# Quantised row tiles of a feed-forward network: transposed by DMA instead of by TensorE and ScalarE, with filler matmuls where TensorE waits

## The reference

```python
x = x + tanh(g_xattn) * xattn(layernorm(x), ctx)          # x is (2, 2048, 512), ctx is (2, 77, 512)
x = x + tanh(g_ffn) * ffn(layernorm(x))

def ffn(x, clip_x, clip_down, w_gate, w_up, w_down):       # w_gate, w_up (1408, 512); w_down (512, 1408)
    xq   = act_fake_quant(x, clip_x)                       # one scale for the whole tensor: needs max |x|
    gate = einsum('bsh,ih->bsi', xq, weight_fake_quant(w_gate))
    up   = einsum('bsh,ih->bsi', xq, weight_fake_quant(w_up))
    h    = act_fake_quant(silu(gate) * up, clip_down)      # one scale again: needs max |silu(gate) * up|
    return einsum('bsi,hi->bsh', h, weight_fake_quant(w_down))

def act_fake_quant(x, clip):
    scale = sigmoid(clip) * max(abs(x)) / 127
    return clip(round(x / scale), -128, 127) * scale
```

## Time and profile before

| | |
|---|---|
| median of 3 runs | 1391.44 us (1388.95 to 1392.56) |
| the profiled execution, its own time | 1387.73 us |
| its span, first to last instruction | 1385.9 us |
| busy: PE / DVE / ACT | 80% / 84% / 91% of the span |
| gate and up, all 8 blocks | about 1136 to 1298 us |
| down | about 1303 to 1382 us |

### The profile page before, as it was taken

How to read it: one execution, slowest core, us unless ns; L and a number is a source line. 1 busy time by engine, 2 the same in 40 slices (tenths; PEclk the granted TensorE clock), 3 DMA queues, 4 the chain that set the end, 5 groups by cost and what they waited for, 6 DMA issues and landing times.

```text
span 1385.9 us, 16773 instructions
## 1 busy us (share of the span) xinstructions
PE 1114.8 (80%) x6868; PEld 348.3 (25%) x6891; DVE 1167.7 (84%) x1679; ACT 1258.5 (91%) x481; POOL 13.9 (1%) x32
## 2 busy tenths in 40 slices
PE   6887678788677787689798798796666659999898
PEld 5321112112111221122122122121111125444343
DVE  7788989986999989778989888777999948888767
ACT  3999999999999999999999999999999956665695
POOL 4000000000000000000000000000000000000000
PEclk9999899999888999899999999999998879999999
DMA  6000011100110001000000100000000013412196
GB/s 222 1 16 1 31 52 56 48 13 16 39 39 23 23 16 36 1 1 1 1 22 22 44 0 1 0 0 0 1 1 0 1 31 130 155 51 62 57 320 238
DMA packets 29872, 61.43 MB, mean 44 GB/s; under 512 B 3771, under 2 KB 5835, under 8 KB 29797
## 3 DMA queue, kind: packets, MB, share of 16 engines
q1 hardware_dynamic: 27840, 59.52, 13.1%
q10 hardware_dynamic: 1253, 0.85, 0.2%
q0 software_dynamic: 704, 0.01, 0.0%
HBM read 46.20 MB, written 14.16 MB: 44 GB/s over the span
## 4 chain that ended last, share of the span: by engine, by line
ACT 72%; PE 19%; DVE 8%; issue 1%; DMA 0%; SPq 0%; DVEq 0%
ACT big L497 71%; PE ps L1164 11%; PE ps L1182 6%; DVE big L687 4%; DVE bn L622 1%; PE ps L981 1%; PE ps L1130 1%; PE ps L1144 0%; DMA wgu<-in_x_dram 0%; PE ps L1040 0%; DVE wgu L630 0%; ACT big L469 0%; ACT big L455 0%; DVE block_sums L730 0%; DVE aux L724 0%
## 5 line engine op out<-in xcount | busy, mean ns | idle before, releaser
L497 ACT ACTIVATE big<-big 128x6144 f32<-128x6144 f32 (+2 forms) x205 | 1062.8, 5322 | 5.0 <-DVE big L687 5.0
L687 DVE TENSOR_SCALAR big<-big,atxt 128x2048 f32<-128x2048 f32 (+2 forms) x918 | 798.6, 922 | 130.2 <-PE ps L1035 117.0
L1035 PE MATMUL ps<-big,wslide 128*32 128x512 f32 x4312 | 613.1, 625 | 190.4 <-ACT big L497 186.9
L1035 PEld LDWEIGHTS ps<-big,wslide 128*32 128x32 f32 x4312 | 131.4, 112 | 611.4 <-ACT big L497 322.6
L1164 PE MATMUL ps<-aux,wgu 128*128 128x512 bf16 x664 | 149.5, 379 | 0.8
L981 PE MATMUL ps<-big,aux 128*128 128x512 f32 x256 | 140.3, 638 | 2.1 <-ACT big L455 2.1
L1040 PE MATMUL ps<-big,wslide 128*32 128x512 f32 x616 | 87.9, 685 | 43.3 <-ACT big L497 43.3
L542 ACT ACTIVATE aux<-ps,sgux 128x512 f32<-128x512 f32 x88 | 59.9, 686 | 56.8 <-PE ps L1164 55.9
L925 DVE SCALAR_TENSOR_TENSOR big<-ps,sgux,aux 128x512 f32<-128x512 f32 x88 | 65.9, 749 | 25.8 <-PE ps L1164 17.3
L1164 PEld LDWEIGHTS ps<-aux,wgu 128*128 128x128 bf16 x680 | 65.3, 98 | 73.4
L1182 PE MATMUL ps<-wd,wgu 128*128 128x512 bf16 x345 | 77.9, 386 | 3.4 <-DVE wgu L941 3.0
(11 more groups left out here) (153 smaller groups left out, 419.5 us busy)
## 6 DMA issues: line engine op xcount, KB each, us to landing
aux<-in_x_dram SPq DMA_DIRECT2D x96, 256.0 KB, 2.7
out_dram<-aux SPq DMA_DIRECT2D x32, 256.0 KB, 3.8
hidden_spill<-big SPq DMA_DIRECT2D x6, 768.0 KB, 5.5
big<-hidden_spill SPq DMA_DIRECT2D x6, 768.0 KB, 8.0
wgu<-in_x_dram SPq DMA_DIRECT2D x11, 256.0 KB, 7.0
aux<-in_L_ffn_w_gate_dram SPq DMA_DIRECT2D x11, 256.0 KB, 2.6
aux<-in_L_ffn_w_up_dram SPq DMA_DIRECT2D x11, 256.0 KB, 2.9
aux<-in_L_ffn_w_down_dram SPq DMA_DIRECT2D x4, 704.0 KB, 4.2
```

Source lines behind the costliest of these rows:

```text
L497: nc.scalar.activation(unit, unit, ACT.Tanh).then_inc(tanh_done, 1)
L687: v.tensor_scalar(ring[:, place(p)], src, atxt[:, e, bt * T + t:bt * T + t + 1], None, ALU.add).then_inc(sums_ready, 1)
L1035: last = mm(bank(k)[32 * part:32 * part + 32, :], wslide[:, e, 31 - g:63 - g], unit[:, part * 512:(part + 1) * 512], start=(e == 0 and g = ...
```

## The change

- Tiles 4 to 31 (blocks 1 to 7) are no longer transposed on TensorE and copied by ScalarE. SP issues one DMA for each, `transpose_in(n)`, from `xq` (128 rows x 512 columns, bf16) straight to `xqT`. Each waits for the tile's `quantise_x`, for the transposing DMA before it (`xqT_in`), and, for a block's first tile, for the block before the last to be multiplied (`up_done`). It stands in SP's list behind the load of tile n + 3, ahead of that turn's store to `hidden_spill`.
- TensorE starts block rb only when the four transposing DMAs of that block have landed (`xqT_in` at 64 rb). `quantise_x(n)` waits for the DMA of tile n - 2 instead of TensorE's transpose.
- `keep_warm(100)` is put between the last attention transpose and the wait for `max_spread`, `keep_warm(40)` behind the transpose of the maximum, `keep_warm(12)` at the end of gate and up, `keep_warm(60)` behind the second transpose of a maximum.
- `alpha_ready` is raised one VectorE instruction earlier; `sgux` has a semaphore of its own.

```diff
             sp.wait_ge(max_ready, BT)
             sp.wait_ge(xn_transposed, TILES)
+            def transpose_in(n):
+                rb, j = n // 4, n % 4
+                sp.wait_ge(xq_ready, n + 1)
+                if n > 4:
+                    sp.wait_ge(xqT_in, 16 * (n - 4))
+                if rb >= 2 and j == 0:
+                    sp.wait_ge(up_done, IC * (rb - 1))
+                sp.dma_start_transpose(xqT[:, rb % 2, :, j * P:(j + 1) * P], xq[:, n % 2, :]).then_inc(xqT_in, 16)
+
             for n in range(TILES):
                 if n >= 3:
                     sp.wait_ge(xu_ready, n - 2)
                 sp.dma_start(xt[:, n % 3, :], x_rows[n * P:(n + 1) * P, :]).then_inc(xt_in[n % 3], 16)
+                if n - 3 >= 4:
+                    transpose_in(n - 3)
                 r, c = n // 4 - 2, n % 4
                 if 0 <= r < SPILLED:
                     sp.wait_ge(h_ready, IC * (r + 1))
                     cut = slice(*cuts[c])
                     sp.dma_start(h_spill[r][:, cut, :], h_slots[:, r, cut, :]).then_inc(h_stored[r], 16)
 
+
+            for n in range(TILES - 3, TILES):
+                transpose_in(n)
...
                     act.wait_ge(gate_done, m + 1)
+                    if m == 0:
+                        act.wait_ge(sgux_ready, 1)
...
-                    if rb + 1 < RB and i in (3, 5, 7, 9):
-                        copy_xqT(4 * (rb + 1) + i // 2 - 1)
...
-            link(v.scalar_tensor_tensor(beta[:, :], mean[:, :], -1.0, alpha[:, :], ALU.mult, ALU.mult))
-            v.tensor_scalar(sgux[:, :, :], sgu[:, :, :], gmax[:, 2:3], None, ALU.mult).then_inc(alpha_ready, 1)
+            v.scalar_tensor_tensor(beta[:, :], mean[:, :], -1.0, alpha[:, :], ALU.mult, ALU.mult).then_inc(alpha_ready, 1)
+            v.tensor_scalar(sgux[:, :, :], sgu[:, :, :], gmax[:, 2:3], None, ALU.mult).then_inc(sgux_ready, 1)
...
             def quantise_x(n):
                 dve.wait_ge(xu_ready, n + 1)
-                if n >= 2:
+                if 2 <= n < 6:
                     dve.wait_ge(xq_transposed, n - 1)
+                if n >= 6:
+                    dve.wait_ge(xqT_in, 16 * (n - 5))
...
             transpose_last()
 
+            keep_warm(100)
             pe.wait_ge(max_spread, 1)
             nc.tensor.transpose(bank(6)[:, 0:P], bcast[:, :], ident[:, :]).then_inc(max_transposed, 1)
+
+            keep_warm(40)
...
             for rb in range(RB):
-                pe.wait_ge(xqT_ready, 4 * (rb + 1))
+                if rb:
+                    pe.wait_ge(xqT_in, 64 * rb)
+                else:
+                    pe.wait_ge(xqT_ready, 4)
...
-                    turns = (4, 5, 7, 9) if rb == 0 else (2, 4, 6, 8)
-                    if rb + 1 < RB and i in turns:
-                        transpose_xq(4 * (rb + 1) + turns.index(i))
+            keep_warm(12)
             pe.wait_ge(max_spread, 2)
             nc.tensor.transpose(bank(6)[:, 0:P], bcast[:, :], ident[:, :]).then_inc(max_transposed, 1)
 
 
+            keep_warm(60)
             pe.wait_ge(hscale_ready, 1)
```

More of the change, by code:

```diff
@@ L179, in flamingo_gated_block @@
         alpha_ready = sem("alpha_ready")
+        sgux_ready = sem("sgux_ready")
         xu_ready = sem("xu_ready")
@@ L214, in flamingo_gated_block @@
         xqT_ready = sem("xqT_ready")
+        xqT_in = sem("xqT_in")
         gate_done = sem("gate_done")
@@ L522, in copy_xqT @@
                 act.wait_ge(xq_transposed, n + 1)
-                if rb >= 2 and j == 0:
-                    act.wait_ge(up_done, IC * (rb - 1))
                 nc.scalar.activation(xqT[:, rb % 2, :, j * P:(j + 1) * P],
@@ L922, in _ @@
                     dve.wait_ge(up_done, m + 1)
+                    if m == 0:
+                        dve.wait_ge(sgux_ready, 1)
                     if rb >= SLOTS and i == 0:
```

## The result

The changed kernel takes 1405.31 us (median of 4 runs, 1404.07 to 1408.54), the kernel before 1390.2 us in the same comparison: a ratio of 1.0116, 95% interval 1.0098 to 1.0133, slower by 15 us. The forecast was 1405 us.

What follows compares the result with a forecast made beforehand. TensorE was taken to bound the FFN, its matmuls and transposes forming each block's chain. Terms -6.2 - 1.4 - 1.8 + 18.8 + 4.4 = +13.8 us, set on the 1391.44 us median, gave 1405 us, range 1399 to 1413.

Steps and rivals of the forecast that it cites:

- two waits at blocks 1 and 2: Tiles 6, 7, 10 and 11 are transposed behind stores, so TensorE waits 9.4 us at each block start: +18.8 us.
- half clock behind them: After each wait at blocks 1 and 2 TensorE works at clock 0.50, losing 2.2 us twice: +4.4 us.
- 28 transposes off TensorE: In gate and up, 28 tiles at 0.22 us each leave TensorE: -6.2 us.
- fillers before the FFN: Filler matmuls between attention and block 0 keep the clock up: gain between 0 and 2.0, taken as -1.4 us.
- fillers before down: Filler matmuls between gate and up and the down matmuls avoid a half-clock start: -1.8 us.
- Hidden elsewhere: In blocks 3 to 7 transposing DMAs, taken at 3.0 us each, hide under the block's matmuls: 0 us.
- The limit of 3.9 us: Longest time per transposing DMA at which four in turn, from 3.5 us on, fit a block's 18.98 us of matmuls.
- fillers that end after the work they wait for: Named sign of a wrong prediction: filler matmuls finishing later than the work they wait for; no size given.
- Slow transposes: Rival, chance 0.18: transposing DMAs take over 3.9 us, so every block waits; about 1424 us at 4.5, 1461 at 5.6.
- the four-times price: Four 128x128 DMA transposes at 1309 ns make 5.2 us a tile; block 24.4 us, whole about 1452 us.
- Short waits: Rival, chance 0.10: transposes overtake stores and land fast at blocks 1 and 2; not slower, 1391 us, or 1382 without waits.

Runs made afterwards that it cites:

- the first experiment: The changed kernel with the eight stores of blocks 0 and 1 moved three turns down SP's list; 1382.32 us, ratio 0.9946 to the kernel before.
- the halves: The changed kernel with stores three turns later, plus each transposing DMA cut into two 256-column DMAs, one after the other; 1437.89 us, ratio 1.0344.

## Why the prediction was right

The sum was +13.8 us; the runs differ by 15.1. Between the two profiled executions, attention left out, it is 17.0. The mechanism was right, but that 1405 met the median to 0.3 us is luck: the sum was set on 1391.44, 1.2 us above the kernel before in the comparison, and in the table below both losses came out larger and both filler gains smaller than forecast. Term by term:

| term | predicted | measured |
|---|---|---|
| two waits at blocks 1 and 2 | +18.8 | +20.7 (10.6 and 10.1) |
| half clock behind them | +4.4 | +5.3: 21.93 - 18.98, and 116.28 - 113.9 over six blocks |
| 28 transposes off TensorE | -6.2 | -6.2 in the first experiment: 680 matmuls and what stands between them in 146.78 us, before from 1144.93 to 1297.91, 152.98 |
| fillers before the FFN | -1.4 | -0.9 (18.2 against 19.1, above) |
| fillers before down | -1.8 | -1.4: from the maximum's transpose to the last matmul 80.2 us (1322.55 to 1402.79), before 81.6 (1300.07 to 1381.70); -1.9 with the fillers alone |

**The waits.** The mechanism was the one named: tiles 6, 7, 10 and 11 behind a store that waits for a whole block. Tile 6 landed 5.2 us after the store was issued (4.9 forecast), tile 7 9.3 (8.5). The rest of the difference is that SP's store left 1.3 us after TensorE ended block 0, not 0.9. The queue's part, which I argued from the load that lands after 4.1 us, is shown by the pair of kernels with and without stores: 7.0 and 10.1 us.

**The clock.** The size taken from the start of down, 2.2 us, was low: 2.95 and 2.4. That it is the clock is shown by block 1 in 19.18 us with fillers in the wait.

**Hidden elsewhere.** Right: 2.5 us in the median, under my 3.0, at most 3.3 away from the stores, and no wait in blocks 3 to 7. The limit of 3.9 us was tested from the other side by the halves, at 4.8.

**The fillers before the FFN.** Here the reason failed and the bounds held. I placed the gain near its upper end "because the wait left over (1129.1 to 1132.85) is under half of the old one". But the clock, still 1.00 in the 3.8 us left over, fell as the next matmuls began, and the 40 fillers took 3.81 us instead of 2.2. They ended at 1140.81, 1.4 us after the first tile was quantised (1139.45), so a sign that I had named for a wrong prediction, "fillers that end after the work they wait for", did come true here; it cost half a microsecond of the sum. With that wait filled they do take 2.4.

**The rivals.** Slow transposes did not happen; the four-times price that I worked out from the Trainium skill's page "VectorE: DVE Perf Modes" (section "The three transpose paths"), 5.2 us, is not what the trace shows: 2.5 us for a tile, 2.3 for half of one, so it does not go by the piece, and the measurement decides. Short waits did not happen either; even with no store data ahead they are 7.0 us, the lower bound I gave (its own numbers, two of 2.4 us from 1161.6 on, make 6.8).

## What to carry to other kernels

A DMA that takes over work from an engine also takes a place in its issuer's list: read what each such place waits for, the store that waits for a whole block above all, before pricing the transfer. Moving those stores three turns turned a loss of 1.2% into a gain of 0.5%. And when filler matmuls are to hold the clock, fill the wait to its end: with a gap of 3.8 us left open they won 0.9 to 1.0 us before the FFN, with the gap closed 2.0.

## What the runs showed of the hardware that I had not expected

- A transposing DMA from SBUF to SBUF with nothing beside it takes 2.4 to 2.5 us for 128x512 bf16 and 2.3 to 2.4 for 128x256: two halves in turn cost nearly twice a whole.
- Its issue takes 1.20 us of SP's time, that of a half 1.17, where a plain load takes 0.33 with the queue empty.
- Behind a 768 KB store and a 256 KB load it lands after 4.2 us. When a packet of the profile's instruction queue starts during its flight it takes 2.9 to 5.5 us, in 18 flights of seven traces; whether the packet is the cause was not tested.
- The unchanged attention stage ends anywhere between 1122.85 and 1127.75 us in profiled executions, so a span alone says nothing below some 5 us.
